# A layer with head attention, causal attention and experts on one core: VectorE sums more products, another order of the front, gates on GpSimd

## The reference, cut to what matters

```python
# s: attention between the 16 heads of one and the same token
q, k, v = ...                      # 16 heads of 8 columns, rope on q and k
att = jnp.einsum('bthd,btgd->bthg', q, k) / jnp.sqrt(jnp.float32(Dh))
att = jax.nn.softmax(att, axis=-1)
out = jnp.einsum('bthg,btgd->bthd', att, v)
...
# f: causal attention over the 8 batches, then a top-2 mixture of 8 experts
scores = jnp.where(causal, scores, jnp.finfo(scores.dtype).min)
...
fc1 = jax.nn.gelu(jnp.einsum('ech,ehf->ecf', xt, moe_w1))
fc2 = jnp.einsum('ecf,efh->ech', fc1, moe_w2).reshape(T, H)
...
x = x + s * g                      # g = silu(f)
```

## Time and profile before

| | us |
|---|---|
| median of 3 runs (lowest to highest) | 598.22 (597.46 to 599.63) |
| the profiled execution's time | 599.06 |
| its span | 597.2 |
| TensorE busy | 411.5 |
| VectorE busy | 369.0 |
| GpSimd busy | 240.7 |
| ScalarE busy | 178.7 |

### The profile page before, as it was taken

One profiled execution on the slowest core, in us unless ns is written; L12 is line 12 of the kernel. 1 busy time (PEld: TensorE's weight loads), 2 busy tenths in 40 slices (PEclk: granted clock), 3 DMA queues, 4 the chain that ended last, 5 costly groups with the idle time before them and its releaser, 6 DMA issues.

```text
span 597.2 us, 4479 instructions
## 1 busy us (share of the span) xinstructions
PE 411.5 (69%) x1404; PEld 239.8 (40%) x1404; DVE 369.0 (62%) x519; ACT 178.7 (30%) x423; POOL 240.7 (40%) x260
## 2 busy tenths in 40 slices
PE   2557747777062559492992967874877679679995
PEld 2545534536020224240441745542655334234442
DVE  6972286987749893989979909942100470741901
ACT  3583724133511000111130755445543110020201
POOL 0883335000078887872000178787777300000000
PEclk9767969879576869688796898776878888989999
DMA  6999000000011011110008231333311350000211
GB/s 171 189 192 298 16 1 1 0 2 1 0 40 36 32 37 45 40 45 13 1 0 231 72 108 35 96 95 107 101 46 44 130 184 0 0 0 2 70 35 35
DMA packets 53541, 38.04 MB, mean 64 GB/s; under 512 B 5321, under 2 KB 50190, under 8 KB 53518
## 3 DMA queue, kind: packets, MB, share of 16 engines
q1 hardware_dynamic: 48910, 28.25, 19.3%
q0 software_dynamic: 4608, 9.51, 4.7%
HBM read 16.55 MB, written 21.20 MB: 63 GB/s over the span
## 4 chain that ended last, share of the span: by engine, by line
PE 32%; DVE 24%; issue 14%; POOL 7%; ACT 3%; DVEq 0%; POOLq 0%
PE banks L833 12%; PE banks L823 7%; POOL expert_rows L1178 5%; DVE prod L260 5%; DVE score L589 4%; PE banks L856 2%; DVE prod L269 2%; DVE prod L257 2%; PE banks L806 2%; PE banks L846 2%; PE banks L844 2%; PE banks L853 1%; ACT flat L1083 1%; PE banks L726 1%; DVE hmax L601 1%
## 5 line engine op out<-in xcount | busy, mean ns | idle before, releaser
L1150 POOL DMA_INDIRECT slot_rows<-rows_all,scatter_at x64 | 88.5, 1383 | 84.3 <-DVE scatter_at L572 65.1
L1178 POOL DMA_INDIRECT expert_rows<-flat,to_at x80 | 85.0, 1062 | 46.4 <-issue 22.6
L833 PE MATMUL banks<-prod,c_identf 128*128 128x512 f32 x192 | 90.9, 634 | 13.6 <-DVE prod L269 13.6
L269 DVE TENSOR_TENSOR prod<-score,qkv_h 128x2048 f32<-128x2048 f32 x24 | 53.9, 2285 | 42.4 <-PE banks L833 38.7
L1137 POOL TENSOR_TENSOR prod<-rows_all,block_kv 128x64 f32<-128x64 f32 (+3 forms) x64 | 48.7, 800 | 50.9 <-DVE score L427 28.1
L823 PE MATMUL banks<-prod,c_identf 128*128 128x512 f32 x112 | 56.2, 661 | 18.8 <-DVE prod L257 18.7
L257 DVE TENSOR_TENSOR prod<-qkv_h 128x2048 f32<-128x2048 f32 x14 | 31.5, 2287 | 53.5 <-issue 53.5
L833 PEld LDWEIGHTS banks<-prod,c_identf 128*128 128x128 f32 x192 | 39.3, 208 | 62.5 <-issue 48.1
L806 PE MATMUL banks<-flat 128*128 128x512 f32 (+1 forms) x96 | 47.4, 655 | 9.3 <-ACT flat L1071 6.3
L260 DVE TENSOR_TENSOR prod<-qkv_h 128x2048 f32<-128x2048 f32 x18 | 40.5, 2291 | 13.7 <-PE banks L823 9.0
L823 PEld LDWEIGHTS banks<-prod,c_identf 128*128 128x128 f32 x112 | 23.7, 216 | 50.3 <-issue 44.9
(11 more groups left out here) (181 smaller groups left out, 594.2 us busy)
## 6 DMA issues: line engine op xcount, KB each, us to landing
slot_rows<-prod SPq DMA_DIRECT2D x10, 528.0 KB, 12.5
flat<-slot_rows SPq DMA_DIRECT2D x16, 264.0 KB, 3.5
expert_rows<-prod SPq DMA_DIRECT2D x8, 512.0 KB, 6.4
flat<-expert_rows SPq DMA_DIRECT2D x8, 512.0 KB, 8.2
xn_all<-in_x SPq DMA_DIRECT2D x4, 512.0 KB, 5.4
flat<-in_w SPq DMA_DIRECT2D x16, 128.0 KB
out<-rows_all SPq DMA_DIRECT2D x8, 256.0 KB, 2.3
expert_rows<-flat,to_at POOLq DMA_INDIRECT x80
```

The costliest lines, as they stand in the source:

```text
L269: return eng.tensor_tensor(value_buf[a].rearrange("p (h g d) -> p h g d", g=H, h=H), p.unsqueeze(3).broadcast_to([P, H, H, HD]), v.rearran ...
L833: i = M.matmul(bank[HEAD_BANK].rearrange("p (a h d) -> p a h d", a=TT, h=H), C["identf"][:], prodB_C.rearrange("p a (h g d) -> p g a h d", ...
L1150: Q.indirect_dma_start(slots_d, bass.IndirectOffsetOnAxis(ap=scatter_at[:, k, n:n + 1], axis=0), z2x[:, h, s, part], None, element_offset= ...
L1178: Q.indirect_dma_start(expert_d, bass.IndirectOffsetOnAxis(ap=to_at[:, e % 2, a:a + 1], axis=0), ye[:, e % 2, a, :], None).then_inc(ye_out ...
```

## The change: what it does

- VectorE sums all score products, and the value products of batches 3 to 7. TensorE sums value products of batches 0 to 2 only, in halves of two blocks (32 products of 256 columns instead of 16 of 512 for a batch). Layouts of q, k and wx follow from that.
- In VectorE's loop both halves of the next batch's scores come before `totals(s)`.
- The order of the front is another on TensorE and ScalarE; `project_heads` of all batches comes after routing.
- The places of `attention_out`, `sum_values` and the exponentials among the experts are others.
- The gates (multiply and add to x) of batches 0 to 5 run on GpSimd.

```diff
-PE_QK = [(0, 0), (1, 0), (2, 0), (6, 0), (6, 1), (7, 0), (7, 1)]
-PE_PV = [0, 1, 2, 5, 6, 7]
+PE_PV = [0, 1, 2]
-EXPONENTIAL_AFTER = {1: 4, 4: 5}
+EXPONENTIAL_AFTER = {0: 3, 2: 4, 5: 5}
+OUT_AFTER = {0: 1, 1: 2, 4: 3, 6: 4}
+POOL_GATES = S - 2
...
 for s in range(S):
     differences(s)
     if s + 1 < S:
         pairs(s + 1, 0)
-    totals(s)
-    values(s, 0)
-    if s + 1 < S:
         pairs(s + 1, 1)
     if s - 1 in PE_PV:
         normalize(s - 1)
+    totals(s)
+    values(s, 0)
     values(s, 1)
     if s not in PE_PV:
         normalize(s)
-for s in range(S - 2):
+for s in range(POOL_GATES, S):
     gated(s)
...
+            value_sums(0)
+            project_rows(2, (1, 0))
+            value_sums(1)
+            turn_normed(0)
+            turn_twice_normed(3)
+            turn_block(0)
+            value_sums(2)
+            project_block(0)
+            project_rows(3, (3, 2))
+            value_sums(3)
+            project_rows(3, (1, 0))
...
-            sum_scores(0, 0)
-            project_heads(2)
...
-            attention_out(3)
-            sum_scores(6, 0)
-            sum_scores(6, 1)
...
+            for s in range(S):
                 project_heads(s)
-            attention_out(2)
+            sum_values(0, 0)
+            sum_values(0, 1)
+            attention_out(0)
+            sum_values(1, 0)
+            sum_values(1, 1)
             pe.wait_ge(W["index_done"], 1)
             pe.wait_ge(W["piece_kept"], len(PIECES))
             for e in range(E):
                 expert(e)
+                if e in OUT_AFTER:
+                    attention_out(OUT_AFTER[e])
+                if e == 0:
+                    sum_values(2, 0)
+                    sum_values(2, 1)
+            pe.wait_ge(W["part_kept"], PARTS * E)
+            for s in range(4):
+                tail_sum(s)
             attention_out(5)
...
+            for s in range(4, POOL_GATES):
                 tail_sum(s)
             attention_out(6)
             attention_out(7)
...
             for e in range(E):
                 expert(e)
+                if e in OUT_AFTER:
+                    keep_attention(OUT_AFTER[e])
                 if e in EXPONENTIAL_AFTER:
                     exponentials(EXPONENTIAL_AFTER[e])
-            keep_attention(3)
             exponentials(6)
-            keep_attention(4)
+            for s in range(4):
+                gates(s)
+            keep_attention(5)
             exponentials(7)
-            keep_attention(5)
...
+            pool.wait_ge(W["tail_in"], 16)
+            for s in range(POOL_GATES):
+                pool.wait_ge(W["silu_done"], s + 1)
+                pool.wait_ge(W["attn_done"], s + 1)
+                Q.tensor_tensor(v_all[:, s, :], v_all[:, s, :], q_all[:, s, :], ALU.mult).then_inc(W["pool_gate"], 1)
+                pool.wait_ge(W["pool_gate"], s + 1)
+                Q.tensor_tensor(xr[:, s], xr[:, s], v_all[:, s, :].rearrange("p (a d) -> p a d", a=TT), ALU.add).then_inc(W["pool_res"], 1)
```

More of the change, by code:

```diff
@@ L593, in differences @@
             def differences(s):
[L594 to L603, removed]
+                src = rows(score[:, s % 2])
+                own(V.tensor_reduce(hmax[:, s % 2], src, AX_X, ALU.max))
+                V.tensor_tensor(src, src, hmax[:, s % 2].unsqueeze(2).broadcast_to([P, TT * H, H]), ALU.subtract).then_inc(W["row_diff"], 1)
             def totals(s):
@@ L624, in normalize @@
                 if s in PE_PV:
[L625 removed]
+                    dve.wait_ge(W["pv_summed"], 2 * PE_PV.index(s) + 2)
                     src = bank[HEAD_BANK]
@@ L688, in _, with project_rows @@
                     turn("z", h, g, zb[:, h % 2])
-                if h == 0:
-                    pe.wait_ge(W["wz_kept"], 1)
-                for j in reversed(range(S // 2)):
+            def project_rows(h, pieces):
+                for j in pieces:
                     k, dst = piece_of("qkv", h, j)
@@ L1034, in _ @@
             A.copy(wpx[:, D:], bank[7][:, 2 * E:3 * E]).then_inc(W["wpx_kept"], 1)
-            for u in range(2 * TT):
-                if 2 <= u + 1 < 2 * TT:
-                    exponentials_of_unit(u + 1)
-                if u >= 2 and u % 2 == 0:
-                    keep_block(u // 2 - 1)
-                if u < TT:
-                    keep_normed(u)
-                if u in (0, 1):
-                    normed(u + 2)
-                if u % 2 == 1 and u + 1 < 2 * TT:
-                    place_values((u + 1) // 2)
-                if u in PX_AFTER:
-                    keep_heads(PX_AFTER[u])
+            exponentials_of_unit(2)
+            keep_qkv(2, (1, 0))
+            place_values(1)
+            twice_normed(3)
+            keep_normed(0)
+            exponentials_of_unit(3)
+            keep_z(3)
+            keep_block(0)
+            normed(1)
+            keep_qkv(3, (3, 2))
+            exponentials_of_unit(4)
+            place_values(2)
+            keep_qkv(3, (1, 0))
+            keep_normed(1)
+            normed(2)
+            exponentials_of_unit(5)
+            keep_block(1)
+            keep_normed(2)
+            normed(3)
+            exponentials_of_unit(6)
+            place_values(3)
+            keep_normed(3)
+            exponentials_of_unit(7)
+            keep_block(2)
             second_roots(0, TT - 1, 1)
@@ L1122, in _ @@
             keep_attention(7)
-            for s in range(S - 2, S):
+            for s in range(POOL_GATES, S):
                 gates(s)
```

159 lines of the change are left out of this document (61 added, 98 removed).

## The result

The changed kernel takes 502.38 us (median of 4 runs, 497.49 to 504.90), the kernel before 598.4: a ratio of 0.838 (95% interval 0.831 to 0.846). Forecast were 489 us and 466 to 518. The profiled execution is the fastest of the four: 497.49 us, span 495.5.

The account below looks back on a forecast made before the run. Bound: VectorE's line plus waits made by the order. First product 141.3 + line 298.7 + waits 16.5, 8 and 8.5 + gate contention 1.5 + end 13.5 = 488.0 us span; 489 us predicted, range 466 to 518.

Parts of the forecast that it names:

- VectorE's line: VectorE's own work without waits, from its first score product through normalizing batch 7: 298.7 us, the longest line.
- three waits: VectorE idle before normalizing batch 2 (16.5 us) and before the totals of batches 5 (8) and 7 (8.5).
- Gain: 31.3 − 8.4 = 22.9 us: Front: VectorE's five waits of 31.3 us shrink to 8.4, so the first score product starts at 141.3.
- Row transfers: GpSimd's 64 indirect transfers, slowed 2.3 us by each of 14 product pairs, end 113.5 us after the first product.
- wait 1: Before normalize(2), VectorE waits 16.5 us for TensorE's sum_values(2), which stands behind expert 0.
- Wait 3: Before totals(7), VectorE waits 8.5 us for exponentials(7), behind expert 7's scatter, tail sums and gates.
- the pace of an expert: GpSimd's time for an expert: 14.63 us with VectorE idle, 19.5 us with VectorE full.
- The end: From the transposes of attention_out(7) to the last output: 13.5 us, unchanged.
- (a): Rival: GpSimd becomes the bound, an expert takes 24 us, 552 us in all; chance 0.06.
- (b): Rival: the front gives nothing, since the pieces that keys need come later, 512 us; chance 0.06.
- (c): Rival: GpSimd's commands are not hindered at all and waits 1 to 3 vanish, 458 us; chance 0.03.
- (d): Rival: GpSimd and VectorE exclude each other both ways, 122 us more, 611 us; chance 0.02.

Follow-up runs that it names:

- sum2_first: Changed kernel with attention_out(1) and both halves of sum_values(2) ahead of expert 0 on TensorE and ScalarE: 494.1 us, ratio 0.824.
- exp_early: sum2_first with exponentials(3) ahead of expert 0, (5) behind expert 4, (7) ahead of the gates: 478.8 us, ratio 0.802.
- vec2: Changed kernel with the value products of batch 2 summed by VectorE too, not by TensorE: 493.0 us, ratio 0.820.
- tail_first: Changed kernel with tail sums and silu of batches 6 and 7 ahead of attention_out(7): 496.9 us, ratio 0.824.
- best1: Changed kernel with keys and values copied to PSUM, batch 6's values summed by TensorE, tail sums and gates ahead of attention_out(7): 443.0 us, ratio 0.737.
- old_front: Changed kernel with the front's order of before on TensorE and ScalarE, head projections still behind routing: 535.7 us, ratio 0.892.
- psum_in: Changed kernel with every product's second input read from 128 unused PSUM columns, so wrong keys and values: 455.5 us, ratio 0.759.

## Why the prediction was right, and where its terms were off

**The bound** was right: VectorE's line (0.7 us off) with three waits, at the places and for the reasons given. sum2_first and exp_early took each away by its place in the order, as the explanation says.

**The total** is in part luck. In the profile the front came 6.5 us earlier than forecast, and the waits and the end were 13.6 us longer (43.0 instead of 33, 17.1 instead of 13.5); so the span is 7.5 us off. The median lies 13.4 us above the forecast, about as much as the waits and the end missed.

**What stays open.** The front and the gates were taken back one at a time (33 us and nothing). The rest, some 63 us, comes from the tables and the order behind the front together: no run has the old tables in the new order, or the reverse.

**"Gain: 31.3 − 8.4 = 22.9 us"**: 29.4 in the profile; place_values(1) and (2) and keep_unit(0) left no wait, the last since TensorE began unit 0's sum at 41.5 instead of the 43.5 to 44 that I placed. But that is at its higher clock. At the lower one the sum began at 44.6 and took 6.9 us instead of 4.19, keep_unit(0) waited 5.7 us, and the first product came at 141.8 (vec2; 141.9 in tail_first). That this is near the forecast 141.3 is luck, as the forecast had no clock in it. It would be most of what parts the profiled 497.5 from the median of 502.4, but the other three executions have no profile, so it isn't shown.

**Row transfers** ended 118.1 us after the first product instead of 113.5. Fifteen pairs of products begin in that stretch, not 14, since the last of them, at 249.75, still met the last command (3.03 us). The surplus is (118.1 − 80.9) / 15 = 2.5 us for a pair, not 2.3: 2.7 for a pair by itself, and 4.3 for four products in a row (L260), which are two pairs. (The prediction's own 80.9 + 14 × 2.3 is 113.1, not 113.5.) So expert 0 started 122.4 us after the first product instead of 118.5, sum_values(2) took 14.0 us instead of 15, and wait 1 was 2.4 us longer.

**Wait 3, 8.5 forecast and 13.9 measured**, is the largest miss behind the front. Expert 5's first command came 240 us after the first product instead of 236, and experts 6 and 7 followed 20.6 and 21.1 us apart where I had 18.5, so that expert 7's scatter ended at 299 us instead of 288.5. VectorE was only 5 us later (308 instead of 303), and the wait grew by the difference. The step that failed is the pace of an expert under a full VectorE: a pair of products mostly costs its commands 3.0 us there (3.05 and 1.90 instead of 0.96 each), not 2.3, and GpSimd's small operation of the gates (L1148), 1.42 us beside a product instead of 0.23, was left out. The prediction also did not keep to its own price: it has 19.5 us for an expert, but steps by 17.5 from expert 1 to 2 and by 18.5 from 5 to 7, without a reason. Only from 4 to 5, where VectorE waited, was the measured step so short (17.7).

**The end, 13.5 forecast and 17.1 measured**: "unchanged" was wrong. Before, TensorE came to attention_out(7) from work; here it had been idle for 16.1 us, and its steps took nearly twice as long (granted clock 0.50), the first of the two tail sums behind among them (1.91 us instead of 1.02 for its first part); the second was back at 1.02. tail_first shows what the sums ahead of it bring, best1 the same steps at the higher clock.

**Rivals.** (a), with GpSimd as the bound, did not decide here, but exp_early stands on it at 479 us: the mechanism was right and its 552 us far too dear. (b) fell with old_front. (c), no hindrance, gives 458 by the sum and 455.5 in psum_in: the line and the waits held, while an earlier first product (135.8) and a longer end (16.6) went against each other; only its condition was not given. (d) fell: products beside commands take 4.49 us. Beside GpSimd's own two-input operations one pair took 5.57, so something like the exclusion that (d) spoke of exists there, once. The front's normalizing at 6.1 us instead of 3.06, where GpSimd's products started first, looks like another case of it, though VectorE's operation is of another kind.

## What to carry to other kernels

A two-input operation of VectorE with both inputs in SBUF (here 128x2048) slows GpSimd's commands for indirect transfers from 0.96 to mostly between 1.9 and 3.1 us; with one input in PSUM it does not, and a spare ScalarE can put it there for 0.6 us. When an order is written by hand, taking one wait away shows the next one: price each wait by its releaser's time and the consumer's, both of which move. The last steps should follow on work of TensorE, not on idleness, and what doesn't depend on the last result belongs ahead of them.

## What was not expected

TensorE's clock from 40 to 50 us was 1.0 in some executions and 0.5 in others of the same front, and the first product came 6 to 7 us later with it where the normalizing took 3.06 us, 1 to 2% of the time. 32 more matrix products before it brought no gain (median 505.5 and 443.7 against 502.4 and 443.0). What decides it stays open. With the second delay, of the normalizing, the first product moved by up to 11.7 us in all.

GpSimd's own 512-element operation took 3.31 us instead of 1.26 beside VectorE's product, far more than the 4.49 against 5.57 that the product lost.
